# The attention units run half by half, and the next stage's first half is normalised before an attention has ended

## The reference

```
h = tok(x)                                    # 16x16 patches, 768 -> 192, plus a position
h = h + attn0(ln(h))   # causal, 12 heads of 16, rotary          (stage 0, "l0a")
h = h + moe0(ln(h))    # 8 experts, top 1, silu-gated            (stage 1)
h = h + grid(ln(h))    # small 3x3 attention                     (stage 2)
h = h + attn1(ln(h))   # 12 heads of 64, q and k normed, gated   (stage 3, "l1f")
h = h + attn2(ln(h))   # has a layer norm of its own inside      (stage 4, "l2a")
h = h + moe2(ln(h))    # 8 experts, top 2, and a shared one      (stage 5)
h = h + attn3(ln(h))   # band mask, 12 heads of 16               (stage 6, "l3a")
h = h + moe3(ln(h))    # 16 experts, top 8, gelu                 (stage 7)
```

## Time and profile before

| | |
|---|---|
| median of 3 runs | 834.84 us (832.56 to 839.68) |
| the profiled execution | 839.98 us, of which 838.3 us are the span of the profile |
| TensorE busy | 769.5 us, 92% |
| VectorE busy | 510.5 us, 61% |
| ScalarE busy | 352.8 us, 42% |
| mean granted TensorE clock | 0.851 of full |

### The profile page before, as it was taken

The page is one execution under the profiler, slowest core; times in us unless marked ns, Lnnn a source line. Parts: engine busy times, 40 slices in busy tenths (PEclk is TensorE's granted clock), DMA queues, the critical chain, the costliest instruction groups (busy, mean ns, idle before and its releaser), DMA issues.

```text
span 838.3 us, 15692 instructions
## 1 busy us (share of the span) xinstructions
PE 769.5 (92%) x6084; PEld 665.6 (79%) x6084; DVE 510.5 (61%) x1348; ACT 352.8 (42%) x808; POOL 64.3 (8%) x53
## 2 busy tenths in 40 slices
PE   6899999999998689899897999899999889979996
PEld 6688869999996266688783688789999757869996
DVE  2546246888878563647624277357877754735775
ACT  0344215545543212467511343145554434526663
POOL 0200000000000302223302000000000030000000
PEclk9865559999999857899885999979999975588999
DMA  9901001224211000000200001011223000102200
GB/s 257 258 2 52 20 1 51 70 76 127 64 52 58 0 1 0 3 1 2 87 2 0 1 4 52 1 39 52 72 86 117 20 1 1 46 2 70 65 20 22
DMA packets 16201, 38.79 MB, mean 46 GB/s; under 512 B 3580, under 2 KB 4572, under 8 KB 15742
## 3 DMA queue, kind: packets, MB, share of 16 engines
q1 hardware_dynamic: 14152, 36.71, 15.0%
q10 hardware_dynamic: 1976, 1.08, 0.5%
HBM read 37.32 MB, written 0.44 MB: 45 GB/s over the span
## 4 chain that ended last, share of the span: by engine, by line
PE 76%; DVE 15%; POOL 3%; ACT 3%; issue 2%; DMA 1%; DVEq 0%; SPq 0%; ACTq 0%
PE PS L687 7%; PE PS L740 6%; PE PS L706 5%; PE PS L528 5%; PE PS L529 4%; PE PS L530 4%; PE PS L531 4%; PE PS L532 4%; PE PS L642 4%; PE PS L676 3%; PE PS L580 2%; PE PS L730 2%; POOL ssq L1638 2%; PE PS L716 2%; PE PS L665 2%
## 5 line engine op out<-in xcount | busy, mean ns | idle before, releaser
L894 ACT ACTIVATE MIX<-PS 128x288 f32<-128x288 f32 x118 | 48.5, 411 | 108.7 <-PE PS L532 108.4
L528 PE MATMUL PS<-XH,WH 128*128 128x288 f32 x284 | 87.1, 307 | 1.1 <-DVE OT L1293 1.0
L529 PE MATMUL PS<-XL,WH 128*128 128x288 f32 x284 | 85.3, 300 | 0.0
L530 PE MATMUL PS<-XH,WL 128*128 128x288 f32 x284 | 85.2, 300 | 0.0
L531 PE MATMUL PS<-X,WH 128*128 128x288 f32 x284 | 85.2, 300 | 0.0
L532 PE MATMUL PS<-X,WL 128*128 128x288 f32 x284 | 85.0, 299 | 0.0
L1293 DVE TENSOR_TENSOR OT<-MIX,PS 128x288 f32<-128x288 f32 x118 | 53.3, 452 | 49.5 <-ACT MIX L894 48.8
L1309 DVE TENSOR_TENSOR AL<-OT,AH 128x288 fp32r<-128x288 f32 x142 | 63.7, 451 | 3.5 <-ACT AH L908 3.0
L908 ACT ACTIVATE AH<-OT 128x288 fp32r<-128x288 f32 x142 | 62.0, 438 | 7.7 <-DVE OT L1301 6.5
L1616 POOL TENSOR_TENSOR rstd<-var,nhalf 96x3 f32<-96x3 f32 x18 | 15.3, 849 | 603.9 <-DVE var L1115 603.9
L580 PE MATMUL PS<-AH,DW 128*128 128x288 f32 x166 | 54.4, 328 | 3.7 <-DVE AL L1309 2.8
(11 more groups left out here) (218 smaller groups left out, 1682.6 us busy)
## 6 DMA issues: line engine op xcount, KB each, us to landing
RG<-in_gu_l0f_dram SPq DMA_DIRECT2D x8, 512.0 KB, 5.4
RG<-in_gu_l0f_dram SPq DMA_DIRECT2D x16, 256.0 KB, 5.6
RG<-in_gu_l2f_dram SPq DMA_DIRECT2D x9, 384.0 KB, 3.8
RG<-in_gu_l2f_dram SPq DMA_DIRECT2D x18, 192.0 KB, 4.2
RD<-in_wd_l0f_dram SPq DMA_DIRECT2D x8, 384.0 KB, 3.3
RD<-in_wd_l2f_dram SPq DMA_DIRECT2D x9, 288.0 KB, 2.9
RD<-in_wd_l3f_dram SPq DMA_DIRECT2D x6, 384.0 KB, 3.1
BIG<-in_patch_dram SPq DMA_DIRECT2D x6, 288.0 KB, 7.4
```

What stands on the lines that cost most here:

```text
L528: mm(o, WH[r][:, 0, w], XH[:, cols], start=True, stop=False)
L529: mm(o, WH[r][:, 0, w], XL[:, cols], start=False, stop=False)
L530: mm(o, WL[r][:, 0, w], XH[:, cols], start=False, stop=False)
```

## The change

A unit is now group `u % ng` and half `u // ng`: all groups of half 0 come first, then all of half 1. As soon as the units of half 0 are mixed and copied (`first_out`), TensorE makes their whole output in one piece: 12 products in A0 and A3, 18 in A1 and A2. One round later VectorE makes `layer_norm(stage + 1, 0)`, within the loop of the attention. Of the output of half 1, two tiles without the last two groups come in round `late == 2` and the third in `late == 3`; then TensorE turns half 0 of the next stage, and last come the 6 products of the last two groups. The two halves of the output change banks of PSUM. In `second_half` the place of `turn(stage, 1)` among the values moves back, in A2 by four pieces, and so do the gates of A1, by one. `evac_xt(k, 0)` now comes before the residual sum of half 1 on VectorE, where it came behind it after the patch, the grid and the attentions. The gates and weights of the mixtures are multiplied on VectorE as before.

```diff
+        self.lag = 1 if token_major else 0
+
+        self.first_out = max(self.ng + self.lag + 4, self.units + 1 if token_major else 0)
+
+    def unit(self, u):
+
+        return u % self.ng, u // self.ng
...
 def second_half(stage, a):
 
-    return a.vpieces - 1 if after_moe(stage) else 2
...
+    return {A0: 3, A1: 4, A2: 6, A3: 3}[a]
...
-        def PB(g):
-
-            return PS[0:TP, (0, 0, 1, 2, 2, 3)[g], (g % TAU % 2) * C:(g % TAU % 2 + 1) * C]
+        def Y(g):
+
+            return PS[0:TP, (2, 2, 3, 0, 0, 1)[g], (g % TAU % 2) * C:(g % TAU % 2 + 1) * C]
...
-                    g, j = u // 2, u % 2
+                    g, j = a.unit(u)
...
-                            if a.gated and p == 5:
+                            if a.gated and p == 6:
                                 gate_logits()
...
-                    late = i - lag - a.units
-                    if 0 <= late < 3:
-
-                        pe.wait_ge(S["o_sb"], u0 + a.units - 4)
-                        output(range(2 * late, 2 * late + 2), range(a.ng - 2))
-                    if late == 3:
-                        pe.wait_ge(S["o_sb"], u0 + a.units - 1)
-                        output(range(TAU), range(a.ng - 2, a.ng)).then_inc(S["y_ready"], 1)
                     if 0 <= i - lag - 4 < a.units:
                         mix(i - lag - 4)
+                    if i == a.first_out:
+
+                        pe.wait_ge(S["o_sb"], u0 + a.ng)
+                        if a.qk_norm:
+                            pe.wait_ge(S["tm_taken"], a.units)
+                        elif a.tm:
+                            pe.wait_ge(S["tm_done"], TM0[a.name] + a.units)
+                        output(range(TAU), range(a.ng)).then_inc(S["y_ready"], 1)
+                    late = i - lag - a.units
+                    if late == 2:
+
+                        pe.wait_ge(S["o_sb"], u0 + a.units - 2)
+                        output(range(TAU, NG - 1), range(a.ng - 2))
+                    if late == 3:
+                        output(range(NG - 1, NG), range(a.ng - 2))
+                pe.wait_ge(S["s_taken"], u0 + a.units)
+                turn(stage + 1, 0)
                 pe.wait_ge(S["o_sb"], u0 + a.units)
                 output(range(TAU, NG), range(a.ng - 2, a.ng)).then_inc(S["y_ready"], 1)
...
-                            if a.gated and p == 6:
+                            if a.gated and p == 7:
                                 router_exp(1, HB * GRP, 128)
...
+            def layer_norm(k, j):
+
+                kind, a = STAGES[k]
+                double = kind == "attn" and a.double_ln
+                n = LN0[k] + (2 if double else 1) * j
+                stream(k, j)
+                if double:
+                    statistics(n, H, j)
+                    link(normalised(n, H, j))
+                    n += 1
+                src = XN if double else H
+                statistics(n, src, j)
+                if j == 1 and kind == "moe":
+                    split_x(a, 0)
+                normalised(n, src, j).then_inc(S["ln_normed"], 1)
+
+            def second_half_in(k):
+
+                kind, a = STAGES[k]
+                if kind != "moe":
+                    evac_xt(k, kind, a, 0)
+                layer_norm(k, 1)
                 if kind != "moe":
                     evac_xt(k, kind, a, 1)
...
+                    if i == a.first_out + 1:
+                        layer_norm(stage + 1, 0)
...
+                if i == 0 or STAGES[i - 1][0] != "attn":
+                    layer_norm(i, 0)
+                second_half_in(i)
```

More of the change, by code:

```diff
@@ L144 @@
 ROUTER = {"l0f": (0, 8), "l2f": (2, 8), "l3f": (3, 16)}
+LN0 = [2 * i + 2 * sum(1 for k, a in STAGES[:i] if k == "attn" and a.double_ln) for i in range(len(STAGES))]
+YN = [sum(1 for k, _ in STAGES[:i] if k != "moe") for i in range(len(STAGES) + 1)]
 XV_N = {"l0a": 0, "l1f": 1, "l2a": 2, "l3a": 3}
@@ L155, in second_half @@
 def second_half(stage, a):
-    return a.vpieces - 1 if after_moe(stage) else 2
-def after_moe(stage):
-    return stage > 0 and STAGES[stage - 1][0] == "moe"
+    return {A0: 3, A1: 4, A2: 6, A3: 3}[a]
 def slot_index(m, s):
@@ L595, in by_tokens @@
                     last.then_inc(S["ysum_ready"], 1)
-                turn(stage, 0, True)
                 router(*ROUTER[m.name], stage, 0)
-                turn(stage, 1, True)
+                turn(stage, 1)
                 router(*ROUTER[m.name], stage, 1)
@@ L739, in output @@
                         for g in groups:
-                            last = mm(PB(t6), tile(OT[0:a.fv, g * B * N:(g + 1) * B * N], t6 // TAU, t6 % TAU), P2[:, g, :],
+                            last = mm(Y(t6), tile(OT[0:a.fv, g * B * N:(g + 1) * B * N], t6 // TAU, t6 % TAU), P2[:, g, :],
                                       start=(g == 0 and t6 % TAU != 1), stop=(g == a.ng - 1), skip_group_check=True)
                     return last
-                lag = 1 if a.tm else 0
-                if not after_moe(stage):
-                    turn(stage, 0)
+                lag = a.lag
                 pe.wait_ge(in_att[a.name], 48)
@@ L811, in grid_attention @@
                         for nd in range(3):
-                            last = mm(PB(g), GT[:, (3 * g + nd) * TP:(3 * g + nd + 1) * TP], wgp[:, nd, :],
+                            last = mm(Y(g), GT[:, (3 * g + nd) * TP:(3 * g + nd + 1) * TP], wgp[:, nd, :],
                                       start=(nd == 0), stop=(nd == 2))
                     last.then_inc(S["y_ready"], 1)
+                turn(stage + 1, 0)
             for k in range(TOKF):
@@ L824, in _ @@
             pe.wait_ge(S["in_first"], 16 * FIRST)
+            turn(0, 0)
             for i, (kind, arg) in enumerate(STAGES):
@@ L1410, in gates, with attention @@
                 last.then_inc(S["gates_made"], 1)
-            def attention(a):
+            def attention(a, stage):
                 u0 = UNIT0[a.name]
```

59 lines of the change are left out of this document (18 added, 41 removed).

## The result

The kernel after takes 811.84 us (median of 4 runs, 810.74 to 816.8), beside 837.26 us for the kernel before on the same chip (832.56 to 841.56). The ratio is 0.971, interval 0.964 to 0.978. That the miss in the time is no larger is partly luck: the forecast started from 834.84, the median of three runs of the kernel before, and its later medians are 839.4 to 841.1, from which the same forecast would be some 826. Run again on another chip, the kernel after took 816.60, inside the range, beside 839.77. Where the runs of a kernel fall into two groups, ratios and their intervals are taken over the quicker group alone, while medians and ranges are over all runs.

What follows compares the result with a forecast made beforehand. TensorE's work at its granted clock, plus its idle time, was taken as the bound. Terms 1.2 - 7.2 + 1.4 - 14.9 + 7 - 1.0 = -13.5, from the median 834.84, gave 821.3 us, range 813 to 832.

Steps and rivals of the forecast that it cites:

- A1 into A2: Border from A1 to A2: `qk` of A2 starts at 451.1 instead of 466.0, a gain of 14.9 us.
- A0 into the first mixture: Border behind A0: the clock rises within the block of 12 products; gain 7.2 us, bounds 0 and 9.4.
- A2: End of A2 into the second mixture: the norm placed before the last `shift` costs time, a loss of 7 us.
- the stall: At A2's end TensorE stands idle for 5.2 us, its next `norm` queued on VectorE behind the moved norm.
- The starts: Starts of A0 and A1: half 1's turn comes later; losses of 1.2 us (0 to 1.5) and 1.4 us.
- the units between the borders: Attention units away from the borders: same work in another order, counted at nothing; clock doubt at most 2.6 us per A0 unit.

Runs made afterwards that it cites:

- The late norm: Kernel after, with A2's norm of the next half 0 made two rounds later, behind the last `norm`: 808.95 us, ratio to before 0.962.
- the shifted kernels: Kernel before with 9, 18 or 27 extra products in the second mixture, ahead of A3: 831.10, 825.24, 834.40 us; kernel after with 18: 827.66 us.
- the repeats: Kernels before and after, each run once more unchanged: 839.68 us and 816.60 us.
- one wait filled: Kernels before and after, each with five unused products ahead of half 1's transposes at A3's start: 831.82 us and 817.09 us.
- both filled: Kernels before and after, with unused products ahead of half 0's (16) and half 1's (five) transposes at A3's start: 831.71 us and 813.42 us.

## Why the prediction was wrong

Its steps, in its order.

- **A1 into A2, -14.9 forecast, -15.7 measured: right.** The clock rose in the block as assumed (somewhere from 423 on; 425 was assumed), the double norm of half 0 was covered, and six pieces at the higher clock reached to the norm of half 1.
- **A0 into the first mixture, -7.2 forecast, -5.5 measured: mechanism right.** The clock rose within the block, 5 to 6 us from its start, as assumed. The block and all behind it came about 6 us later than I had put them (97.15 instead of 91.2), partly because A0's start was slower.
- **A2, +7 forecast, +6.9 measured: right**, with the stall at 4.96 us (5.2 forecast), and the lower clock behind it for part of the way. The late norm confirms the stall's cause; it gave back 3.6 us, the price of the stall alone. That the low clock follows from the stall, as the sum had it, is not shown: it was low there with a wait of 1.24 us too.
- **The starts: mis-sized.** A0's came out at +3.4 where 1.2 was forecast and 1.5 was the bound. The later `turn` adds a third piece; the three took 6.98 us, nearly all at the lower clock, where two had taken 3.60. I had priced the added piece at the higher one. The place of `turn` does not explain all of it: the seven profiles with the new place have 14.5 to 15.3 us here, but of the eleven with the old one seven have 11.9 to 12.9 and four 14.2 to 15.3. So A0's start has two values by the clock as well. A1's start gained 1.9 where a loss of 1.4 was forecast and a gain of up to 1 was allowed; what followed gave 1.6 of it back.
- **The step that failed: "the units between the borders do the same work in another order and are counted at nothing … Doubt about their clock is at most 2.6 for each A0 unit that has its level changed."** The work is indeed the same. But A3's units took 46.0 us instead of 62.4. These 16.4 us are more than the 14.7 by which the profiles' difference (28.2) exceeds the forecast. The clock of a whole stretch of units hangs in large part on where it falls at the start, so the doubt was not some 2 us but 18 us between the best A3 (44.3) and the worst (62.4). I had taken A3's low clock as a given, and no row of before was shown for it.

The fallacy can be named: I treated the clock at A3 as a property of A3. The change did not touch the instructions from the second mixture to A3's scores, so I left the stage out. What the change did touch was the instant at which they run, and by the shifted kernels that is enough.

How much of the 25 us is then the order's own? In these profiles, 11.8 us of 28.2 lie outside A3; in those of the repeats it is 12.5, with one wait filled in both kernels 8.1, with both filled 16.5. The medians are 14.7 us apart with one wait filled (831.82 and 817.09) and 18.3 with both (831.71 and 813.42). So an estimate from these numbers is that 8 to 18 us are the order's, which has the 13.5 of the forecast in it, and the remaining 7 to 17 are where A3's clock falls. That part is not a merit of the change: 18 added products took it from the kernel after in three of four runs, and gave it to the kernel before in nine of ten.

Left open is what ties the clock's changes to the program's time so well that ten executions of a shifted kernel agree, while 25 of the kernel before spread over 825 to 850 (and over 822 to 848 on other chips). That the instant decides is thus supported by the shifts and by the profiles, and why it does is not known. It was not tried to shift other stages; A1's units too vary, from 89.6 to 97.0 us over kernels that have them in the old order and from 92.8 to 98.5 in the new one.

## What to carry to other kernels

Where TensorE's granted clock changes level near a stage with small products, its level there is a term of the sum with two values, not a constant of the stage: work out both, and give the difference over the whole stage to the range, also for stages that the change does not touch. Before a gain is put down to an edit, shift the same stage by a few us of harmless work, take some ten runs of each kernel, and see whether the gain survives. Short waits ahead of small products are the place to look: fill them with work that is needed anyway, as the six pieces do at A2; products of no use kept the clock from falling there, but made a kernel quicker by 1.2% at most (the kernel before with one wait filled), and with both waits filled by nothing clear of the noise. And keep a long norm out of the queue ahead of an instruction that TensorE waits for.

## What was not expected of the hardware

- Added work can make a kernel quicker: 18 products, 2.1 us, turned 840.3 us into 825.2 in the median, by making the slow outcome rare and not by passing the best runs of the kernel before (825.22).
- At the lower clock TensorE can be busy without a gap and stay there: 30.00 us of 30 busy at 0.50 in A3 before. It rose while dense blocks ran: 12 output products in A0 (low at 97 to 102, 0.81 at 102 to 104, then 1.00), and three value pieces in A3 after. The Trainium skill has in "TensorE: Matmul & The Clock Gate", part 1, that activity releases the throttle; if a busy share were activity, A3 before would be against it. The same part of the Trainium skill's page has it that the gate's timing runs free of the kernel and the outcome varies from run to run. The kernel before agrees (825 to 850 us), and the shifted ones hardly do (nine of ten runs within 3.2 us).
- In the kernel before a fall to the lower level that lasted 51 us came 1.8 us behind an idle time of 2.2 us, and an idle time of the same length passed without one in the same profile, 8 us earlier (the wait for half 0, with the clock at 1.00 from 673 to 681). With both filled there was no fall at this place. Within A3's units falls followed waits of 1.0 to 1.4 us.
